# Products of the identity in TensorE's waits at stage borders of a 12-stage fused network, and two memsets moved behind a layer norm

## The reference

```
x = x + _L0_xattn_ref(_layernorm(x), ctx_768, ...)    # 16 heads
x = x + _L0_attn_ref(_layernorm(x), ...)              # 16 heads, relative bias
x = x + _L0_ffn_ref(_layernorm(x), ...)               # quantised to 4 bits
x = x + _L1_xattn_ref(_layernorm(x), ctx_768, ...)
x = x + _L1_attn_ref(_layernorm(x), ...)              # one head
x = x + _L1_ffn_ref(_layernorm(x), ...)               # low rank, below
x = x + _L2_xattn_ref(_layernorm(x), ctx_768, ...)
x = x + _L2_attn_ref(_layernorm(x), ...)              # a scan
x = x + _L2_ffn_ref(_layernorm(x), ...)               # experts with a capacity
x = x + _L3_xattn_ref(_layernorm(x), ctx_768, ...)    # below
x = x + _L3_attn_ref(_layernorm(x), ...)              # one head
x = x + _L3_ffn_ref(_layernorm(x), ...)               # top experts
```

```
def _L1_ffn_ref(x, W, b, V_r, C):
    base = jnp.einsum('bsd,od->bso', x, W) + b
    correction = jnp.einsum('bsr,or->bso', jnp.einsum('bsd,dr->bsr', x, V_r), C)
    return base + correction

def _L3_xattn_ref(modality1, modality2, ...):
    x1 = layernorm(modality1, ln1_g, ln1_b)
    x2 = layernorm(modality2, ln2_g, ln2_b)
    q, k, v = x1 @ Wq + bq, x2 @ Wk + bk, x2 @ Wv + bv
    scores = jnp.einsum('bqe,bke->bqk', q, k) * scaling
    attn = jax.nn.softmax(scores, axis=-1)
    return jnp.einsum('bqk,bke->bqe', attn, v) @ Wo + bo
```

## Time and profile before

| what | value |
|---|---|
| median of 3 runs | 1903.74 us (1898.66 to 1909.04) |
| profiled execution, its own time | 1909.2 us |
| its span in the trace | 1907.0 us, 35283 instructions |
| TensorE busy | 1602.8 us (84%), 12373 products |
| VectorE / ScalarE / GpSimd busy | 1125.1 (59%) / 822.1 (43%) / 761.8 us (40%) |
| granted TensorE clock, mean | 0.911 of full speed |

### The profile page before, as it was taken

How to read it: one execution, slowest core, us unless ns; L and a number is a source line. 1 busy time by engine, 2 the same in 40 slices (tenths; PEclk the granted TensorE clock), 3 DMA queues, 4 the chain that set the end, 5 groups by cost and what they waited for, 6 DMA issues and landing times. The chain is left out here.

```text
span 1907.0 us, 35283 instructions
## 1 busy us (share of the span) xinstructions
PE 1602.8 (84%) x12373; PEld 1358.6 (71%) x12373; DVE 1125.1 (59%) x3117; ACT 822.1 (43%) x2394; POOL 761.8 (40%) x927
## 2 busy tenths in 40 slices
PE   6999999666868999976999999699869477739996
PEld 6899889434547999846889998646569334528995
DVE  5887876488746888644767767459721322432222
ACT  4666666113326888712666666320123022113332
POOL 6666565352329999513211111147532111030111
PEclk9999999878979999987999999999879777859998
DMA  8545543200032333206233333160152573911112
GB/s 259 178 147 179 167 150 130 76 1 1 0 120 79 129 127 137 68 19 195 95 108 106 119 107 130 69 208 1 50 184 83 137 202 116 360 45 40 40 34 86
DMA packets 139710, 213.70 MB, mean 112 GB/s; under 512 B 19450, under 2 KB 106434, under 8 KB 139058
## 3 DMA queue, kind: packets, MB, share of 16 engines
q1 hardware_dynamic: 132418, 199.50, 32.5%
q0 software_dynamic: 3408, 8.54, 1.3%
q10 hardware_dynamic: 3712, 3.41, 0.6%
HBM read 170.07 MB, written 47.78 MB: 114 GB/s over the span
## 5 line engine op out<-in xcount | busy, mean ns | idle before, releaser
L802 DVE TENSOR_SCALAR xattn_oT<-bank,xattn_last 128x256 f32<-128x256 f32 x256 | 111.7, 478 | 90.7 <-PE bank L623 90.6
L708 ACT ACTIVATE xattn_probs<-bank,xattn_negmax 128x257 f32<-128x257 f32 x256 | 123.7, 483 | 65.6 <-DVE xattn_negmax L783 65.5
L713 ACT ACTIVATE xattn_probs<-xattn_probs,xattn_rsum 128x257 f32<-128x257 f32 x256 | 131.8, 515 | 1.4 <-DVE xattn_rsum L787 1.4
L1028 POOL TENSOR_SCALAR xattn_probs<-xattn_probs,xattn_rsum 128x257 f32<-128x257 f32 x128 | 119.5, 934 | 22.8 <-DVE xattn_rsum L1263 22.8
L783 DVE TENSOR_REDUCE xattn_negmax<-bank 128x1 f32<-128x257 f32 x256 | 106.4, 416 | 34.9 <-PE bank L596 33.4
L792 DVE TENSOR_TENSOR xattn_probsT_lo<-bank,xattn_probsT_hi 128x256 fp32r<-128x256 f32 x256 | 104.9, 410 | 9.8 <-ACT xattn_probsT_hi L719 8.7
L603 PE MATMUL bank<-ident,xattn_probs 128*128 128x128 f32 x512 | 103.9, 285 | 7.1 <-ACT xattn_probs L713 6.7
L719 ACT CAST xattn_probsT_hi<-bank 128x256 fp32r<-128x256 f32 x256 | 95.4, 373 | 32.3 <-PE bank L603 28.2
L541 POOL COPY ctx_stat<-xattn_mv 128x2 f32<-128x2 f32 x32 | 6.0, 187 | 237.7 <-DVE xattn_mv L816 237.7
L592 PE MATMUL bank<-xattn_ctxT,xattn_qk_hi 128*128 128x258 f32 x256 | 93.8, 366 | 0.5 <-DVE xattn_qk L779 0.5
L2121 POOL TENSOR_TENSOR scan_product<-scan_state,scan_qT 128x512 f32<-128x512 f32 x64 | 75.6, 1182 | 36.2 <-DVE scan_state L2258 35.8
(11 more groups left out here) (503 smaller groups left out, 5297.0 us busy)
## 6 DMA issues: line engine op xcount, KB each, us to landing
xattn_ctxT<-ctx_partsT SPq DMA_DIRECT2D x64, 516.0 KB, 3.9
xattn_ctxN<-ctx_partsN SPq DMA_DIRECT2D x64, 384.0 KB, 4.4
ctx_partsT<-xattn_ctxT SPq DMA_DIRECT2D x32, 516.0 KB, 2.7
moe_w<-in_L_ffn_W SPq DMA_DIRECT2D x16, 1024.0 KB, 13.7
ctx_partsN<-xattn_ctxN SPq DMA_DIRECT2D x32, 384.0 KB, 3.6
moecap_w_early<-in_L_ffn_w SPq DMA_DIRECT2D x10, 1024.0 KB, 13.1
xattn_rawN<-in_ctx SPq DMA_DIRECT2D x32, 192.0 KB, 2.7
xattn_raw<-in_ctx SPq DMA_DIRECT2D x32, 192.0 KB, 4.4
```

The costliest lines, as they stand in the source:

```text
L708: nc.scalar.activation(probs[:, n % RING, :], SB[n % 2][:, 0:KV], ACT.Exp, bias=negmax[:, n % RING:n % RING + 1], accum_out=psum[:, n % RI ...
L713: nc.scalar.mul(probs[:, n % RING, :], probs[:, n % RING, :], rsum[:, n % RING:n % RING + 1]).then_inc(norm_ready, 1)
L802: nc.vector.tensor_scalar(oT[k][:, heads, b, :], by_head(OB[:, k * 2 * P:(k + 1) * 2 * P]), last[:, k, j * PER_TILE + b:j * PER_TILE + b + ...
L1028: nc.gpsimd.tensor_scalar(probs[:, n % RING, :], probs[:, n % RING, :], rsum[:, n % RING:n % RING + 1], None, ALU.mult).then_inc(norm_read ...
```

## The change

A new method, `Core.keep_busy(n, bank)`, issues n products of the identity, read as 16-bit numbers: 128 rows times 256 columns each, into a PSUM bank that the stage overwrites afterwards with a start of its own. Nothing reads them. It is called with

- 34 at the start of low_rank, 20 at the start of attn1 and of attn3 each, 16 at the start of xattn3, 40 at the start of xattn1;
- 20 (attn1) and 38 (attn3) between the scores and the wait for the turned probabilities;
- 22 in xattn1 between the wait for the second half of `xnT` and the loop, 60 in fp4 between the weights' turns and the first tile's;
- 12 in xattn3 ahead of every scores(t) but the first, and 8 ahead of every turn_probs(t). In scores the wait for the loaded `T` goes behind the 12, in turn_probs the wait for the probabilities behind the 8.

That is 418 products. In attn0 GpSimd's wait for all eight normalised tiles moves ahead of its two memsets, and VectorE's one wait for all eight bias adds ahead of its evictions becomes a wait for the tile's own, ahead of the last add of each tile (L1546).

```diff
--- before.py
+++ after.py
@@ -36,6 +36,12 @@
         self.partsT = nc.dram_tensor("ctx_partsT", (BATCH, P, 2, 2, KV + 1), F32, kind="Internal").ap()
         self.partsN = nc.dram_tensor("ctx_partsN", (BATCH, P, 2, 3 * P), F32, kind="Internal").ap()
         self.bank = [ctx.enter_context(nc.psum_tensor(f"bank{i}", [P, 512], F32)) for i in range(8)]
+
+    def keep_busy(self, n, bank):
+
+        same = self.ident[:, :].bitcast(BF16)
+        for _ in range(n):
+            self.nc.tensor.matmul(self.bank[bank][:, 0:2 * P], same[:, 0:P], same[:, 0:2 * P], start=True, stop=True)
 
 
 class Stage:
@@ -179,6 +185,7 @@
 
         @block.tensor
         def _(pe):
+            core.keep_busy(34, 7)
             pe.wait_ge(loaded, 16 * LOADS)
             for c in range(CD):
                 nc.tensor.matmul(core.bank[4 + c][:, 0:D], vT[:, c * P:(c + 1) * P], cT[:, :], start=True, stop=True).then_inc(vc_done, 1)
@@ -1143,6 +1150,7 @@
                     mm = nc.tensor.matmul(M2[:, 0:D], aT[:, c, :], wo_s[:, c, :], start=(c == 0), stop=(c == CD - 1))
                 mm.then_inc(m2_filled, 1)
 
+            core.keep_busy(40, 7)
             for c in range(CD):
                 keys(0, c)
             ln.pe(pe, 0)
@@ -1150,6 +1158,7 @@
             queries(0)
             ln.pe(pe, 1)
             pe.wait_ge(ln.xnT_ready, 2 * CD)
+            core.keep_busy(22, 7)
             for t in range(ALL + UNITS):
                 j, s = divmod(t, UNITS)
                 if 0 <= t - TURN < ALL:
@@ -1383,10 +1392,10 @@
         @block.gpsimd
         def _(pool):
             ln.pool(pool)
+            pool.wait_ge(ln.xn_ready, TILES)
             nc.gpsimd.memset(v[:, :, :, :], 0.0).then_inc(v_zero, 1)
             nc.gpsimd.memset(probsT[:, :, :, :], 0.0).then_inc(probsT_zero, 1)
             pool.wait_ge(loaded, 16 * LOADS)
-            pool.wait_ge(ln.xn_ready, TILES)
             for t in range(TILES):
                 nc.gpsimd.tensor_tensor(core.x[:, t, :], core.x[:, t, :], bo[:, :], ALU.add).then_inc(bo_added, 1)
             for s in range(TILES + SUM):
@@ -1500,7 +1509,6 @@
             ln.dve(dve)
             step = Chain(dve, steps)
             dve.wait_ge(loaded, 16 * LOADS)
-            dve.wait_ge(bo_added, TILES)
             for k in range(8):
                 n, f = divmod(k, 4)
                 dve.wait_ge(qk_done, k + 1)
@@ -1542,6 +1550,7 @@
                     last.then_inc(probsT_ready, 1)
                 if s >= ADD:
                     t = s - ADD
+                    dve.wait_ge(bo_added, t + 1)
                     dve.wait_ge(y_done, t + 1)
                     nc.vector.tensor_tensor(core.x[:, t, :], core.x[:, t, :], bank[6 + t % 2][:, 0:D], ALU.add).then_inc(x_done, 1)
 
@@ -1618,6 +1627,7 @@
 
         @block.tensor
         def _(pe):
+            core.keep_busy(20, 7)
             ln.pe(pe)
             pe.wait_ge(loaded, 16 * LOADS)
             for n in range(2):
@@ -1646,6 +1656,7 @@
                         mm = nc.tensor.matmul(S[b * SEQ:(b + 1) * SEQ, t * SEQ:(t + 1) * SEQ], qT[:, c, own], kT[:, c, own],
                                               start=(c == 0), stop=(c == CD - 1), tile_position=(0, b * SEQ))
             mm.then_inc(scores_done, 1)
+            core.keep_busy(38 if soft_theta else 20, 5)
             pe.wait_ge(probsT_ready, 1)
             for s in range(TILES + (2 if soft_theta else 0)):
                 if s < TILES:
@@ -1935,6 +1946,7 @@
                 for k, source in enumerate(sources):
                     mm = nc.tensor.transpose(bank[n % WBANKS][0:rows, k * P:(k + 1) * P], source, core.ident[:, :])
                 mm.then_inc(turned, 1)
+            core.keep_busy(60, 4)
             turn_x(0)
             for s in range(TILES + 2):
                 if s < TILES:
@@ -3245,9 +3257,11 @@
             def scores(t):
                 z = t % RING
                 pe.wait_ge(qk_ready, 2 * (t // 4 + 1))
-                pe.wait_ge(T_loaded[z], (t // RING + 1) * 48)
                 if t >= 2:
                     pe.wait_ge(scaled_ready, t - 1)
+                if t >= 1:
+                    core.keep_busy(12, t % 2)
+                pe.wait_ge(T_loaded[z], (t // RING + 1) * 48)
                 for b in range(PER_TILE):
                     r, q = slice(b * SEQ, (b + 1) * SEQ), slice(t * P + b * SEQ, t * P + (b + 1) * SEQ)
                     nc.tensor.matmul(SB[t % 2][r, 0:KV], qk1[:, q], T1[:, z, b, :], start=True, stop=False, tile_position=(0, b * SEQ))
@@ -3255,9 +3269,10 @@
                 mm.then_inc(scores_done, 1)
 
             def turn_probs(t):
-                pe.wait_ge(probs_ready, t + 1)
                 if t:
                     pe.wait_ge(probsT_ready, 2 * t)
+                core.keep_busy(8, 2)
+                pe.wait_ge(probs_ready, t + 1)
                 for c in range(KCH):
                     nc.tensor.transpose(TB[:, c * P:(c + 1) * P], probs[:, t % 2, c * P:(c + 1) * P], core.ident[:, :])
                 mm = nc.tensor.transpose(TB[0:1, KCH * P:(KCH + 1) * P], probs[:, t % 2, KCH * P:KV], core.ident[:, :])
@@ -3312,6 +3327,7 @@
                                               start=(c == 0), stop=(c == CD - 1))
                 mm.then_inc(y_done, 1)
 
+            core.keep_busy(16, 7)
             ln.pe(pe, 0)
             queries(0)
             ln.pe(pe, 1)
```

## The result

| | before | changed |
|---|---|---|
| median of 13 runs each | 1907.03 us (1898.66 to 1918.07) | 1896.53 us (1893.56 to 1905.34) |
| ratio, 95% interval | | 0.9945 (0.9926 to 0.9964) |
| span of the profiled execution | 1907.0 us | 1897.8 us |
| mean granted clock there | 0.911 | 0.931 |

What follows compares the result with a forecast made beforehand. The prediction saw TensorE's clock halved in stretches where a stage starts or TensorE had waited, some on the path. Terms of -3.0 - 3.3 - 2.0 - 0.4 - 0.3 - 1.0 - 6.0 = -16.0 took 1903.7 to 1887.7 us, range 1878 to 1901.

Steps and rivals of the forecast that it cites:

- Rival D: Whole kernel: the products raise the clock nowhere and cost 0.21 us each; about +20 us, median 1924; chance 0.08.
- rival C: xattn3's loop: its products cost 0.21 us each and buy no clock; +11.7 us there, median 1905.4; chance 0.07.
- attn0, -3.0: attn0: moving the memsets ends VectorE's stall, projections begin 4.7 us earlier, half clock takes 1.7 back; -3.0 us.
- attn1 and low_rank, -5.7 together: Full clock in low_rank -3.3 us, at attn1's products with the values -2.0, at attn1's head -0.4.
- fp4 and xattn1, -1.3: Products in waits: fp4's first turn of x faster, -0.3 us; xattn1, -1.0 us.
- xattn3, -6.0: xattn3: the loop's chain at full clock gains 7.6 us, less 1.6 for products ahead of scores(t); -6.0 us.
- The step of scores(5): xattn3, scores(5) to the reload's release: 6.9 us instead of 9.85, eight products included; 2.9 us less.
- the step of scores(3): xattn3, an earlier step of the chain, partly at full clock already; 1.2 us less.
- the step of scores(7): xattn3, the chain's later step, same work as that of scores(5); 2.9 us less again.
- attn3, 0: attn3: its gain is hidden, as moe's start waits for a load; 0 us (0 to -2).
- A: Whole kernel, the forecast itself: the products hold the clock at most borders; median 1887.7 us; chance 0.58.
- B: Whole kernel: clock falls before the real work; only attn0, low_rank and attn1's values gain; -8.3 us, median 1895.4; chance 0.27.

Runs made afterwards that it cites:

- no_loop: The changed kernel without the 12 and 8 products per tile in xattn3's loop, the 16 at its head kept; ratio to before 0.9940.
- memsets_only: The kernel before with only attn0's memsets and bias-add wait moved, no products of the identity; ratio to before 0.9957.
- loop_double: The changed kernel with 24 and 16 products per tile in xattn3's loop in place of 12 and 8; ratio to before 0.9983.
- loop_half: The changed kernel with 6 and 4 products per tile in xattn3's loop in place of 12 and 8; ratio to before 0.9926.
- no_attn1_low_rank: The changed kernel without the 20 and 20 products in attn1 and the 34 in low_rank; ratio to before 0.9945.
- pared: The changed kernel without the products in fp4 (60), xattn1 (40 and 22) and attn3 (20 and 38); ratio to before 0.9929.
- xattn3_only: The kernel before with xattn3's products alone (16 at its head, 12 and 8 a tile); ratio to before 0.9982.
- products_only: The kernel before with all 418 products, attn0 left as it was; ratio to before 0.9958.
- attn0_filled: The changed kernel with 30 more products at attn0's head and 16 between its transposes and its wait for loads; ratio to before 0.9935.
- combined: The changed kernel with attn0's 46 products added and those of fp4, xattn1 and attn3 left out; median 1895.03 us, ratio to before 0.9923.
- xattn2_filled: The changed kernel with 34 more products at xattn2's head and 10 between its first transposes and its queries; ratio to before 0.9939.

## Why the prediction held, and where its sum was off

**Direction and mechanism: right.** The question on which all rivals stood was whether the products hold the clock. In most places they do: low_rank, attn1's values and the middle of xattn3 run at 1.00, a product costs 0.112 to 0.118 us, and a quarter-wide one holds the clock as well. Rival D (they don't, 1924 us) and rival C (xattn3's loop buys no clock) are out. That 1560 to 1573 stood at 0.50 with TensorE busy all the time had spoken for D; no_loop shows the same, and the loop's products end it.

**attn0, -3.0: right mechanism, too small.** The stall went, the loads set the start 6.5 us after the issue of the last, and half clock took part of it back, step by step as forecast. Measured over all kernels it is -5.0. The loss by the clock was taken as certain (1.7), but in three of the nine kernels with the move and without attn0's own products (memsets_only, loop_double, loop_half) the clock had risen in time: there the stage is 7.1 us shorter on average, in the six others 4.0. In these three the last projection ends 5.5 us earlier, 4.7 by the earlier start and 0.8 because the kernel before had run its own first projections partly at half clock (2.67 us for four against 1.98); the rest comes later in the stage and is not traced. That this term brought 2.0 us more than forecast hides as much of what the others lacked; so far the time of the whole came near by luck.

**attn1 and low_rank, -5.7 together: gain smaller, and given back.** In the changed kernel's profile it was -5.4, over all kernels -3.3: attn1 -2.0 (forecast -2.4), low_rank -1.3 (forecast -3.3). So low_rank is the term that was mis-sized. The load of low_rank landed 0.9 us later against the stage's start than assumed, and in five of ten kernels the clock fell once in low_rank between 6 and 10 us after its start in spite of the products; it took 18.2 us in these and 16.7 in the other five, against 18.7 without products. One step is missing from the sum altogether: the stage behind. xattn2 was 2.4 us longer on average, and no_attn1_low_rank has the same time as the changed kernel, within 5 us either way. The sum took every microsecond gained at a border as gained for the whole.

**fp4 and xattn1, -1.3: not to be measured.** -1.1 between means whose members spread over 4 us; pared lost nothing. That GpSimd's spread sets a wait in xattn1 the prediction saw, and still it put 1.0 us on the clock there.

**xattn3, -6.0: step right, stage -4.4, whole less.** The step of scores(5), 6.9 forecast, took 6.2 in all nine kernels with 12 and 8 (9.5 to 9.8 in the three without). The stage's first half was not free: from its start to scores(4) it was 46.7 us instead of 44.7, and 46.0 to 49.7 in the nine against 43.0 to 46.3 in the three. Transfers run at a DMA share of 1.0 to 1.1 from 12 to 35 us after the stage's start, with the products or without, and the first probs_ctx came 1.2 us later than before; which of the two set the delay is not shown. By means, nine kernels against three, scores(5) comes 1.6 us later (the sum had 0.4, as 1.6 for the products less 1.2 for the step of scores(3)), from there to scores(7) it is 3.7 shorter (forecast 2.9), and the tail is 2.3 shorter (forecast 3.5: 2.9 for the step of scores(7), 0.6 for what follows); no_loop has that gain without the loop's products. 12 products ahead of every scores(t) and 8 ahead of every turn are close to the bound: doubling them cost 7 us of the whole. The stage's mean is 97.8 us with them (nine kernels) and 102.2 without (three), but the time of the whole shows 3.4 us in xattn3_only and none in no_loop. How much of the 4.4 the loop's products are worth stays open between 0 and 4.

**attn3, 0: right**, hidden behind moe's loads.

**The sum** of the stages' means, -5.0 - 1.1 - 3.3 + 2.4 - 4.4 = -11.4, agrees with -10.5 measured. Against -16.0 the largest differences are the giving back in xattn2 (2.4), attn1 and low_rank (2.4) and xattn3 (1.6), with attn0 (2.0) the other way. The result lies between A and B, nearer to B's -8.3. The sentence of the Trainium skill (TensorE: Matmul & The Clock Gate, "What's actually happening") that the ramp penalty is under 1% of a typical kernel span is not tested by these runs: 418 products in eleven places brought 0.4% by themselves (products_only), which is under 1%, but the mean granted clock there was still 0.930, so what all the half clock of the kernel costs was never measured. The clock's mean of 0.911, which the prediction set beside that sentence, speaks neither for rival B nor against it.

**What stays open.** Why the falls of the clock in xattn2 lie where they do. The first begins 1.0 to 1.6 us after the stage's start in seven of the eight executions that took 355.1 us or more, and 1.8 to 2.8 in those that took 352.5 to 353.6; one more fall in the tail, some 342.5 us after the start, is in all eight longer ones and in none of the six shorter; a second fall of 6.8 us or more, against 3.4 in the kernel before, is in all eight and in two of the six (attn0_filled and combined). The changed kernel loses 1.5 us against before at the second fall and 1.7 at the one in the tail. Eight of the ten kernels with low_rank's products are among the longer ones, the other two have products in attn0 too, and none of the four without; why is not shown, and xattn2_filled excludes only the head.

## What to carry to other kernels

Work that nobody needs can hold TensorE's clock up through a wait, but it pays only where TensorE's next work is on the path and starts soon after; behind a transfer or a busy GpSimd it brought nothing here that could be measured, and in a loop whose waits are short it soon became the bound itself. Count on less than the border's gain for the whole: look at the next stage too, and compare several executions, as one pair of traces differs by some microseconds in stages that nobody changed. A memset on GpSimd that runs beside VectorE's normalising is worth moving first: here it gave as much as all the products.

## What the runs showed of the hardware

- A product with 32 columns of weights holds the clock as one with 128 does (mean clock 0.933 and 0.932 over the timed runs).
- Two memsets of GpSimd, 3.50 us each and back to back, held one normalise of VectorE through both: it took 7.03 us, the others 0.40 to 0.41. Moved behind the normalises, the memsets held up no eviction from PSUM: in memsets_only an eviction at 367.59 lies inside the second memset and takes 0.75 us, as long as the later ones.
- The mean clock is no measure of what was gained. Over 35 runs of the kernel before, time falls by 1.2 us for every 0.001 of mean clock (correlation -0.82), so about two thirds of the variation between one execution and another goes with the clock. The changed kernel has 0.022 more than before, which by that would be 25 us; it is 10.5 us faster. Clock that is granted to waits and to the products themselves gains nothing, which is plainest in loop_double: 0.934 and only 0.2% faster than before.
